# A decoder layer on one core: Toeplitz tiles from zero-padded rows, 128-partition loads, statistics on ScalarE, warm-up products

## The chip, the cores and the metric

One core of a Trainium2 chip runs the whole program. The metric is the device time of one execution in microseconds.

## The reference

x has 4 sequences of 1024 tokens with 256 channels. One pre-norm decoder layer is computed in fp32: a state-space mixer, a cross-attention to 64 context rows, and a feed-forward block with two hidden products of 1024 by 1024. The change touches the mixer alone:

```python
xn = (x - mu) / jnp.sqrt(var + LN_EPS) * ln_gamma + ln_beta   # x is itself layer-normed
dA = jnp.exp(-jnp.exp(log_A) * dt[:, None])                    # 256 channels x 64 states
dB = B_param * dt[:, None]
def step(h, u):
    h = dA * h + dB * u[..., None]
    y = jnp.einsum('dn,bdn->bd', C_param, h) + D_param * u
    return (h, y)
```

The kernel does the scan over time in 16 chunks of 64 tokens. Within a chunk a channel's output is a 64 by 64 lower-triangular Toeplitz matrix times the chunk; between chunks the 64 states are carried.

## The kernel before

Names: tok holds the normed input, 128 partitions (two halves of 64 times, one for each half of the channels) by 64 chunks by 128 channels. GG holds the powers of dA times B times C, built by six doublings on VectorE (L337). EE holds exp of alpha times the position, for the entries into a state. TT, four buffers in the tensor ring, holds Toeplitz tiles of 16 channels each: 64 partitions a half, partition p being the row of kernel values shifted by p.

The rows of kernel values come from TensorE (L461): ones times GG, in four rounds of two banks, evacuated by ScalarE into ksb (L277), stored to DRAM as kernel_rows (L175), 64 values for each of 256 channels, one channel behind the other. tt_load (L141) reads them back for group g, one transfer for each half of the partitions. Since the rows stand close together, the upper triangle holds the next channel's values, and GpSimd sets it to zero (mask, L211, two selects a group). entries_load (L146) reads the alpha rows to all 64 partitions of a half, again one transfer a half.

Order on the queues. SP issues, in program order: coefficients, x in its natural layout (xres), alpha rows out, x by chunks (tok), gamma and beta, EE groups 0 and 1, bo and woT, the eight kernel-row stores (each waits for its evacuation), the later weights' first ones, TT groups 0 to 3, EE groups 2 to 7. TT groups 4 to 7 follow in sync_core, each when the products of a buffer are done; then the feed-forward weights. VectorE does the coefficients, the doublings with statistics (bn_stats, bn_aggr) of x between them, the edit of two rows of GG by D (L397) and its undoing (L411), the norms of 24 of 64 chunks (L370; ScalarE does 40, L284), gamma and beta in eight parts (L379, L384, z_b counts the betas). GpSimd does constants, the powers (1/sqrt), the selects, later the bias.

TensorE's mixer loop runs 17 steps o over 16 octets of 8 channels. Step o does the state products of octet o+1 (L470, EE), the within products of octet o (L477, TT), and the carried products of octet o-1 (L484, GG and the scan of VectorE, L431). It starts with z_b of 3 (L486); at each even step it waits for the mask of a new TT group (L494). The output is evacuated by ScalarE (L304), which between these does the EE exponentials (L289) and the residual's base (L292). Projection, attention and the feed-forward loop of eight blocks follow; none of their lines is changed.

Of the kernel before, what the change touches and what calls it, by code (L numbers as in the profile page):

```python
# [32 lines left out]
P = 128  # L33
# [21 lines left out]
ACT_SHARE = 20  # L55
# [3 lines left out]
def mixer_parts(nc, ctx, a, t):  # L59
# [7 lines left out]
    def sem(name):  # L67
# [12 lines left out]
    ones = sb("ones", [P, 32], "c")  # L80
# [33 lines left out]
    kps = [[pair[k][:, 512 * h:512 * (h + 1)] for h in range(2)] for k in (2, 0)]  # L114
# [5 lines left out]
    const, exps, coef, al_st, coef_t, pk_done, g_row, d_add = (  # L120
        sem("m_" + n) for n in ("const", "exps", "coef", "al_st", "coef_t", "pk_done", "g_row", "d_add"))
    k_ps, k_ev, kr_pad, e_rdy, t_mask = (sem("m_" + n) for n in ("k_ps", "k_ev", "kr_pad", "e_rdy", "t_mask"))
    kr_st = sem("m_kr_st")
    T_in = [sem(f"m_T_in{k}") for k in range(4)]
    stat, aggr, sv_rdy, powd, shift, spr, z_rdy, z_dve, z_h, z_b, natural, nat_v = (
# [13 lines left out]
    def tt_load(e, g):  # L139
        for h in range(2):  # L140
            e.dma_start(TT[g % 4][L * h:L * h + L, :],  # L141
                        bass.AP(t["kr_h"], (8 * h + g) * (GRP * L), [[1, L], [1, GRP * L]])).then_inc(T_in[g % 4], 16)

    def entries_load(e, g):
        for h in range(2):
            e.dma_start(EE[L * h:L * h + L, GRP * g:GRP * g + GRP, :].rearrange("p d n -> p (d n)"),  # L146
                        bass.AP(t["alS_h"], (8 * h + g) * (GRP * N), [[0, L], [1, GRP * N]])).then_inc(E_in[g], 16)

    def sync_mixer(e):
# [20 lines left out]
        for v in range(4):  # L170
            for h in range(2):
                u = 2 * v + h
                e.wait_ge(k_ev, u + 1)
                c = (1 - h) * (P * L) + v * 2048
                e.dma_start(kr[0, c:c + 2048].rearrange("(q m) -> q m", q=4), ksb[0:P:32, u, :]).then_inc(kr_st, 16)  # L175
        for n in ("xW", "keys", "scl"):
            e.dma_start(t[n], a[n]).then_inc(k_in, 16)
        e.wait_ge(kr_st, 128)
        e.wait_ge(kr_pad, 16)
        for g in range(4):  # L180
            tt_load(e, g)
        for g in range(2, NGRP):
            entries_load(e, g)
# [22 lines left out]
    def mask(e, g):  # L206
        e.wait_ge(T_in[g % 4], 32 * (g // 4 + 1))
        for h in range(2):
            e.wait_ge(t_mask, 2 * g + h)
            v = TT[g % 4][L * h:L * h + L, :].rearrange("p (d t) -> p d t", d=GRP)  # L210
            e.affine_select(out=v, in_=v, compare_op=ALU.is_ge, fill=0.0, base=L - 1,  # L211
                            pattern=[[0, GRP], [-1, L]], channel_multiplier=-1).then_inc(t_mask, 1)

# [4 lines left out]
    def gpsimd_prep(e):  # L218
        e.memset(ident[:, :], 0.0).then_inc(const, 1)
        e.memset(rev[:, :], 0.0).then_inc(const, 1)  # L220
        e.memset(ones[:, :], 1.0).then_inc(const, 1)
# [4 lines left out]
        e.wait_ge(const, 6)  # L226
        e.affine_select(out=ident[:, :], in_=ident[:, :], compare_op=ALU.not_equal, fill=1.0, base=0,
                        pattern=[[-1, P]], channel_multiplier=1).then_inc(const, 1)
        for h in range(2):
            blk = rev[64 * h:64 * h + 64, 64 * h:64 * h + 64]  # L230
            e.wait_ge(const, 7 + h)
            e.affine_select(out=blk, in_=blk, compare_op=ALU.not_equal, fill=1.0, base=-63,
                            pattern=[[1, 64]], channel_multiplier=1).then_inc(const, 1)
        e.wait_ge(const, 9)
        e.dma_start(kr[:, DM * L:DM * L + L], rev[0:1, L:2 * L]).then_inc(kr_pad, 16)

        for b in range(2):
# [3 lines left out]
        mask(e, 0)  # L241
        e.wait_ge(t_mask, 2)
        e.wait_ge(nat_v, 1)
        e.tensor_tensor(rsm[:, :], svn[:, :], mhalf[:, :], ALU.pow).then_inc(natural, 1)
        e.wait_ge(natural, 1)
        for g in range(1, 4):
            mask(e, g)
        e.wait_ge(t_mask, 8)

    def gpsimd_core(e):  # L250
        e.wait_ge(wo_in, 32)
        done = 0
        for g, until in ((4, 0), (5, 0), (6, 0), (7, 4), (None, TILES)):
            for tile in range(done, until):
                bias(e, tile)
            done = until
            if g is not None:
                e.wait_ge(base_b, done)
                mask(e, g)
                e.wait_ge(t_mask, 2 * g + 2)  # L260

    def scalar(e):
# [11 lines left out]
        def row_evac(v):  # L274
            e.wait_ge(k_ps, v + 1)
            for h in range(2):
                e.activation(ksb[:, 2 * v + h, :], kps[v % 2][h], ACT.Copy).then_inc(k_ev, 1)  # L277
# [8 lines left out]
        def entry_exp(g):  # L286
            e.wait_ge(E_in[g], 32)
# [5 lines left out]
        for v in range(4):  # L293
            row_evac(v)
        e.wait_ge(const, 9)
        norm_apply(0)
        entry_exp(0)
        norm_apply(1)
        for g in range(1, 3):
# [21 lines left out]
    def vector(e):  # L321
        e.wait_ge(exps, 2)
# [8 lines left out]
        for row in (0, N):  # L331
            e.tensor_copy(edit[row:row + 1, 1, :], wT[row:row + 1, :]).then_inc(d_add, 1)
# [6 lines left out]
        def stats(first, until):  # L339
            for j in range(first, until):  # L340
                if j % 4 == 0:
                    e.wait_ge(xr_in[j // 4], 16)
                e.bn_stats(stn[:, j, :], xres[:, j, :]).then_inc(stat, 1)
                if j % SB >= 2:
                    e.wait_ge(stat, j - 1)
                    e.bn_aggr(mvn[:, j - 2, :], stn[:, j - 2, :]).then_inc(aggr, 1)

        def variances(b):
            for j in (SB * b + SB - 2, SB * b + SB - 1):
                e.wait_ge(stat, j + 1)  # L350
                e.bn_aggr(mvn[:, j, :], stn[:, j, :]).then_inc(aggr, 1)
            e.wait_ge(aggr, SB * b + SB)
# [37 lines left out]
        stats(4, 8)  # L390
        double(5)
        e.wait_ge(d_in, 32)
        e.wait_ge(d_add, 2)
        e.wait_ge(g_row, 7)
        for row in (0, N):
            v = GG[row:row + 1, :, L - 1]
            e.tensor_tensor(v, v, edit[row:row + 1, 0, :], ALU.add).then_inc(d_add, 1)  # L397
        stats(8, 16)
        variances(0)
        stats(16, 26)  # L400
        spreads(0)
        stats(26, 32)
        variances(1)
        e.tensor_scalar(svn[:, :], mvn[:, :, 1], EPS, None, ALU.add).then_inc(nat_v, 1)
        for k in range(2):
            e.memset(hps[k], 0.0).then_inc(h_zero, 1)
        norms(0)
        spreads(1)
        e.wait_ge(k_ps, 4)
        for row in (0, N):  # L410
            e.tensor_copy(GG[row:row + 1, :, L - 1], edit[row:row + 1, 1, :]).then_inc(g_row, 1)  # L411
        e.memset(dec[:, :, 0], 0.0).then_inc(dec0, 1)
        e.wait_ge(bc_in, 64)
        gamma(0)
        norms(1)
        beta(0)
        gamma(1)
        beta(1)
        gamma(2)
# [28 lines left out]
    def tensor(e):  # L448
        e.wait_ge(const, 9)
# [1070 lines left out]
```

## Time and profile before

| what | us |
|---|---|
| median of 3 runs (lowest, highest) | 941.73 (940.8, 942.72) |
| the profiled run's own time | 942.65 |
| its span | 940.9 |
| TensorE matmul busy | 869.4 (92%) |
| VectorE busy | 524.6 (56%) |
| ScalarE busy | 494.1 (53%) |
| GpSimd busy | 184.0 (20%) |

The busy shares are means over stages with different limits. The mixer fills the first 104 us of the span, projection with the first block's attention the next 60, and the feed-forward loop the rest. PE is TensorE's matmul, PEld its weight load, DVE VectorE, ACT ScalarE, POOL GpSimd, SP the engine that issues transfers; a q behind a name is that engine's sequencer. A busy PE is not PE at its peak, since matmuls are pipelined.

### The profile page before, as it was taken

What the parts mean: (1) busy time and instruction counts of PE and PEld (TensorE: products, weight loads), DVE (VectorE), ACT (ScalarE), POOL (GpSimd) and SP (SyncE); (2) the same over time, 40 slices, a digit from 0 to 9 for tenths busy, and PEclk for the clock granted to TensorE, in tenths of its full rate; (3) what the DMA queues carried; (4) which work ended last, traced back from release to release, by engine and by line L of the source; (5) the groups of instructions that cost most, each with busy time, mean ns of one, the idle gap of its engine ahead of it and who ended that gap; (6) DMA issues with size and microseconds to landing.
All of it is one profiled execution on the core that took longest, in us unless ns stands there. A gap on an engine that the chain in (4) does not pass through costs nothing.

```text
span 940.9 us, 15107 instructions
## 1 busy us (share of the span) xinstructions
PE 869.4 (92%) x5570; PEld 695.4 (74%) x5570; DVE 524.6 (56%) x927; ACT 494.1 (53%) x761; POOL 184.0 (20%) x201
## 2 busy tenths in 40 slices
PE   1169899999999999999999999999999999999996
PEld 0068767777877777777777777778777877777885
DVE  7987486646456545646455555555655465544411
ACT  2827533675356635663575446653675357635331
POOL 1667700500050004100220023000500050003000
PEclk9669999999999999999999999999999999999998
DMA  9962797500110011000200020001000110001000
GB/s 346 242 152 52 270 396 280 224 1 1 51 45 0 0 50 45 0 0 22 72 0 0 5 90 0 0 0 64 31 0 0 50 45 0 0 23 46 0 1 24
DMA packets 15496, 61.77 MB, mean 66 GB/s; under 512 B 2835, under 2 KB 4502, under 8 KB 14646
## 3 DMA queue, kind: packets, MB, share of 16 engines
q1 hardware_dynamic: 15430, 61.31, 19.0%
q8 instruction: 23, 0.38, 0.2%
q14 instruction: 11, 0.09, 0.0%
q0 software_dynamic: 32, 0.00, 0.0%
HBM read 49.63 MB, written 23.20 MB: 77 GB/s over the span
## 4 chain that ended last, share of the span: by engine, by line
PE 85%; DVE 7%; issue 4%; ACT 2%; POOL 0%; DMA 0%; DVEq 0%; SPq 0%; ACTq 0%; POOLq 0%
PE pair L1196 50%; PE pair L1183 9%; PE pair L1208 6%; PE pair L1123 4%; PE pair L1134 3%; PE pair L1150 3%; PE pair L470 2%; DVE nat L885 2%; PE pair L1143 1%; PE pair L1173 1%; PE pair L477 1%; PE pair L1090 1%; PE pair L539 1%; PE pair L484 1%; DVE GG L337 1%
## 5 line engine op out<-in xcount | busy, mean ns | idle before, releaser
L806 ACT ACTIVATE vbuf<-pair,scl 128x512 f32<-128x512 f32 x128 | 87.6, 684 | 231.2 <-PE pair L1196 222.3
L1196 PE MATMUL pair<-h2hi,h_turned 128*128 128x512 f32 x512 | 202.6, 396 | 0.0
L1196 PE MATMUL pair<-h2lo,h_turned 128*128 128x512 f32 x512 | 199.6, 390 | 0.0
L1196 PE MATMUL pair<-h1hi,h_turned 128*128 128x512 f32 x384 | 153.1, 399 | 0.0
L1196 PE MATMUL pair<-h1lo,h_turned 128*128 128x512 f32 x384 | 149.9, 390 | 0.0
L973 DVE TENSOR_TENSOR h1lo<-vbuf,h1hi 128x512 fp32r<-128x512 f32 x80 | 57.8, 722 | 119.2 <-ACT h1hi L807 118.4
L1196 PEld LDWEIGHTS pair<-h2hi,h_turned 128*128 128x128 f32 x512 | 96.2, 188 | 25.2 <-issue 5.9
L1196 PEld LDWEIGHTS pair<-h2lo,h_turned 128*128 128x128 f32 x512 | 96.2, 188 | 19.3
L973 DVE TENSOR_TENSOR h2lo<-vbuf,h2hi 128x512 fp32r<-128x512 f32 x64 | 44.2, 691 | 107.2 <-ACT h2hi L807 107.1
L997 DVE SCALAR_TENSOR_TENSOR vbuf<-pair,scl,sg 128x512 f32<-128x512 f32 x64 | 47.4, 748 | 81.7 <-ACT sg L795 69.0
L1183 PE MATMUL pair<-zThi,w_turned 128*128 128x512 f32 x224 | 91.2, 407 | 0.4 <-DVE vbuf L997 0.4
L1196 PEld LDWEIGHTS pair<-h1hi,h_turned 128*128 128x128 f32 x384 | 72.1, 188 | 24.5 <-issue 10.5
L1183 PE MATMUL pair<-zTlo,w_turned 128*128 128x512 f32 x224 | 87.6, 391 | 0.0
L759 ACT ACT_TABLE_LOAD x65 | 83.4, 1283 | 1.2
L700 POOL TENSOR_TENSOR lnv<-lnv 128x4 f32<-128x4 f32 x16 | 16.2, 1015 | 345.1 <-DVE lnv L878 320.4
L1196 PEld LDWEIGHTS pair<-h1lo,h_turned 128*128 128x128 f32 x384 | 72.2, 188 | 14.1
L732 POOL TENSOR_TENSOR h1lo<-vbuf,h1hi 128x512 fp32r<-128x512 f32 x48 | 62.5, 1302 | 82.3 <-ACT h1hi L798 82.3
L795 ACT ACTIVATE sg<-pair,scl 128x512 f32<-128x512 f32 x64 | 43.9, 686 | 58.4 <-PE pair L1183 57.2
L470 PE MATMUL pair<-tok,EE 64*64 64x60 f32 x512 | 38.7, 279 | 26.8 <-DVE tok L384 24.9
L1183 PEld LDWEIGHTS pair<-zThi,w_turned 128*128 128x128 f32 x224 | 42.0, 188 | 15.1 <-DVE vbuf L997 5.0
L714 POOL TENSOR_TENSOR kblk<-keys,hmask 128x256 f32<-128x256 f32 x18 | 10.7, 615 | 207.6 <-PE pair L1123 207.6
L1196 PE MATMUL pair<-h1hi,w_turned 128*128 128x512 f32 x128 | 50.4, 394 | 0.0
(145 smaller groups left out, 1604.3 us busy)
## 6 DMA issues: line engine op xcount, KB each, us to landing
h_turned<-d_h SPq DMA_DIRECT2D x2, 4096.0 KB, 15.0
xres<-in_x SPq DMA_DIRECT2D x8, 512.0 KB, 7.0
tok<-in_xs SPq DMA_DIRECT2D x8, 512.0 KB, 12.1
EE<-alpha_rows SPq DMA_DIRECT2D x16, 256.0 KB, 11.0
ring<-kernel_rows SPq DMA_DIRECT2D x16, 256.0 KB, 4.4
xr<-x_rows SPq DMA_DIRECT2D x8, 512.0 KB, 3.4
out<-xr SPq DMA_DIRECT2D x16, 256.0 KB, 2.1
x_rows<-xres SPq DMA_DIRECT2D x7, 512.0 KB, 11.3
```

Source lines behind the costliest of these rows:

```text
L470: ins = e.matmul(out, EE[L * h:L * h + L, i, :], rhs, start=True, stop=True)
L732: e.tensor_tensor(h1[1][:, m, :], vb[:, m % 2, :], h1[0][:, m, :], ALU.subtract).then_inc(S["lo"], 1)
L759: e.activation(warm[:, 1:2], warm[:, 0:1], function).then_inc(S["warm"], 1)
L795: e.activation(sg[:, m % 2, :], pair[m % 2][:, 0:512], ACT.Silu, scale=sc1[:, m:m + 1]).then_inc(S["sg_rdy"], 1)
L806: e.activation(vb[:, s % 2, :], h_ps[s % 4], ACT.Gelu, scale=sc)
L973: e.tensor_tensor(dst[1][:, n % HC, :], vb[:, n % 2, :], dst[0][:, n % HC, :], ALU.subtract).then_inc(S["lo"], 1)
L997: e.scalar_tensor_tensor(vb[:, m % 2, :], pair[m % 2][:, 512:1024], sc2[:, m:m + 1], sg[:, m % 2, :], ALU.mult, ALU.mult).then_inc(S["v_rd ...
L1123: ins = e.matmul(pair[2][:, g * BLK + b * 256:g * BLK + (b + 1) * 256], qa[64 * g:64 * g + 64, h, tile * P:(tile + 1) * P], kblk[64 * g:64 ...
L1134: ins = e.transpose(pair[3][:, b * BLK + r * P:b * BLK + (r + 1) * P], unit(j, u)[:, r // 2, c:c + P], ident[:, :])
L1183: ins = e.matmul(pair[m % 2][:, 512 * g:512 * g + 512], w[:, k, m * P:(m + 1) * P], zT[part][:, k * BLK:(k + 1) * BLK], start=(k == 0 and ...
L1196: ins = e.matmul(bank, w[:, k, m * P:(m + 1) * P], src[part][:, k, :], start=(k == 0 and part == 0), stop=(k == HC - 1 and part == 1))
L1208: ins = e.matmul(h_ps[m], h1T[:, k, m * P:(m + 1) * P], h1[part][:, k, :], start=(k == 0 and part == 0), stop=(k == HC - 1 and part == 1))
```

## The change

The DRAM rows become 128 values wide (PAD), 64 kernel values and 64 zeros, so that a Toeplitz tile read with a shift of one a partition has its zeros from memory. The selects are gone, and so is their place in GpSimd's later work. The zeros are written once, by four transfers from rev. Each Toeplitz and each EE load is one transfer to 128 partitions whose DRAM side has the counts 2, 64 and the row. Toeplitz tiles grow to 8 KB a partition; two of the four buffers lie in the place of w1 and w2, ksb in that of w3, so the loads of these weights wait for the last within products. The kernel rows are summed over the four rounds into one pair of banks, through a matrix (pick) that has ones in one column, so that round v lands on row v of each block of 32. ScalarE computes mean and variance of tiles 8 to 15 of x by two passes with a summed output each; VectorE does the other 24. The row edits of GG go to GpSimd, their saved copy to ScalarE. Two memsets of banks and one of dec go to the start of VectorE's program. ScalarE does 36 norms and VectorE 28, and norms(1) stands behind gamma and beta of two parts. After the second beta TensorE does five 128x512 products that nothing reads.

```diff
-ACT_SHARE = 20
+ACT_SHARE = 18
+ACT_STATS = (8, 16)
+ROWS_AT = 8
+PAD = 2 * L
...
+    TT = [ring[:, 0:GRP * PAD], ring[:, GRP * PAD:2 * GRP * PAD]]
+    TT += [nc.alloc_sbuf_tensor_at(f"tt{k}", [P, GRP * PAD], F32, offset=t[n])[:, :] for k, n in enumerate(("w1_at", "w2_at"))]
+    ksb = nc.alloc_sbuf_tensor_at("ksb", [P, 2, BLK], F32, offset=t["w3_at"])
...
     def tt_load(e, g):
-        for h in range(2):
-            e.dma_start(TT[g % 4][L * h:L * h + L, :],
-                        bass.AP(t["kr_h"], (8 * h + g) * (GRP * L), [[1, L], [1, GRP * L]])).then_inc(T_in[g % 4], 16)
+        e.dma_start(TT[g % 4], bass.AP(t["kr_h"], g * (GRP * PAD), [[8 * GRP * PAD, 2], [1, L], [1, GRP * PAD]])).then_inc(T_in[g % 4], 16)
 
     def entries_load(e, g):
-        for h in range(2):
-            e.dma_start(EE[L * h:L * h + L, GRP * g:GRP * g + GRP, :].rearrange("p d n -> p (d n)"),
-                        bass.AP(t["alS_h"], (8 * h + g) * (GRP * N), [[0, L], [1, GRP * N]])).then_inc(E_in[g], 16)
+        e.dma_start(EE[:, GRP * g:GRP * g + GRP, :].rearrange("p d n -> p (d n)"),
+                    bass.AP(t["alS_h"], g * (GRP * N), [[8 * GRP * N, 2], [0, L], [1, GRP * N]])).then_inc(E_in[g], 16)
...
+        e.wait_ge(const, 10)
+        for u in range(4):
+            e.dma_start(kr[0, L * u * PAD:L * (u + 1) * PAD].rearrange("(c m) -> c m", m=PAD)[:, L:PAD], rev[0:L, L:P]).then_inc(kr_zero, 16)
         e.wait_ge(al_st, 32)
         for g in range(2):
             entries_load(e, g)
+        for h in range(2):
+            e.wait_ge(k_ev, h + 1)
+            for v in range(4):
+                c = (P * (1 - h) + 32 * v) * PAD
+                e.dma_start(kr[0, c:c + 32 * PAD].rearrange("(q c m) -> q c m", q=4, c=8)[:, :, 0:L],
+                            ksb[v:P:32, h, :].rearrange("q (c m) -> q c m", c=8)).then_inc(kr_st, 16)
+        entries_load(e, 2)
+        e.wait_ge(kr_st, 128)
+        e.wait_ge(kr_pad, 16)
+        e.wait_ge(kr_zero, 64)
+        for g in range(2):
+            tt_load(e, g)
+        entries_load(e, 3)
+        for g in range(2, 4):
+            tt_load(e, g)
+        for g in range(4, NGRP):
+            entries_load(e, g)
...
         e.wait_ge(w_d, 48)
+        e.wait_ge(w_ps, NOCT)
...
+        for row in (0, N):
+            v = GG[row:row + 1, :, L - 1]
+            e.tensor_tensor(v, v, edit[row:row + 1, 0, :], ALU.add).then_inc(d_add, 1)
+        e.wait_ge(d_add, 2)
+        power(0)
+        e.wait_ge(k_ps, 1)
+        e.wait_ge(powd, 1)
+        for row in (0, N):
+            e.tensor_copy(GG[row:row + 1, :, L - 1], edit[row:row + 1, 1, :]).then_inc(g_back, 1)
+        e.wait_ge(g_back, 2)
+        power(1)
...
+        def tile_stats(first, until):
...
+            for j in range(first, until):
+                e.activation(junk[j % 4], xres[:, j, :], ACT.Copy, accum_out=tsum[:, 0, j:j + 1]).then_inc(t_sum, 1)
+            e.wait_ge(t_sum, n)
...
+            for j in range(first, until):
+                e.activation(junk[j % 4], xres[:, j, :], ACT.Square, bias=tsum[:, 1, j:j + 1], scale=1.0 / 16, accum_out=mvn[:, j, 1:2]).then_inc(t_var, 1)
...
+                if c == ROWS_AT:
+                    row_evac()
...
+            if b == 0:
+                e.wait_ge(t_var, ACT_STATS[1] - ACT_STATS[0])
+            e.wait_ge(aggr, ACT_STATS[0] + SB * b)
...
+                    ins = e.matmul(kps[h][32 * q:32 * q + 32, :], pick[N * h:N * h + N, 3 - v:35 - v], GGf[N * h:N * h + N, c:c + 8 * L], start=(v == 0), stop=(v == 3))
+        ins.then_inc(k_ps, 1)
+        e.wait_ge(pk_done, 7)
+        e.wait_ge(w_row, 2)
+        e.wait_ge(z_b, 2)
+        for _ in range(5):
+            e.matmul(pair[3][:, 0:BLK], ident[:, :], GGf[:, 0:BLK], start=True, stop=True)
...
-                e.wait_ge(t_mask, o + 2)
+                e.wait_ge(T_in[o // 2 % 4], 16 * (o // 8 + 1))
```

## Rows read from the trace of the kernel before

**Rows 1.** The page's slices: granted clock and DMA share, in 40 equal slices.
```profile
PEclk9669999999999999999999999999999999999998
DMA  9962797500110011000200020001000110001000
```

**Rows 2.** The chain in order of time: start us, us, what; 0 to 110.
```profile
14.95 4.32 DVE GG L337
...
37.46 1.23 DVE tok L379
...
39.85 1.06 issue
...
46.99 2.17 DVE tok L379
49.19 2.05 DVE tok L384
51.28 1.86 PE pair L470 x30
...
56.64 3.27 issue
```

**Rows 3.** Groups by line, 0 to 104: busy us, mean ns | idle before, releasers.
```profile
L211 POOL TENSOR_SCALAR_AFFINE_SELECT ring<-ring 64x1024 f32<-64x1024 f32 x16 | 24.1, 1508 | 16.5 <-DMA ring<-kernel_rows 15.5
...
L292 ACT ACTIVATE xres<-xres,ngn,rsn 128x256 f32<-128x256 f32 x32 | 17.0, 591 | 0.0
...
L343 DVE BATCH_NORM_STATS2 stn<-xres 128x6 f32<-128x256 f32 x32 | 12.4, 401 | 0.1
...
L370 DVE TENSOR_SCALAR tok<-tok,spread 128x128 f32<-128x128 f32 x24 | 7.9, 406 | 0.0
...
L406 DVE MEMSET pair<- 128x512 f32 x2 | 1.0, 485 | 0.2
...
L397 DVE TENSOR_TENSOR GG<-GG,edit 1x128 f32<-1x128 f32 x2 | 0.8, 404 | 0.2
...
L411 DVE COPY GG<-edit 1x128 f32<-1x128 f32 x2 | 0.6, 300 | 0.1
```

**Rows 4.** Busy time by stretch: us, engines, granted clock, DMA share, GB/s.
```profile
10.00:20.00 10.00, 0.00 (x0) 0.00 (x0) 9.84 (x18) 0.00 (x0) 0.00 (x0) 1.00 1.03 409
50.00:57.00 7.00, 5.35 (x155) 5.13 (x156) 6.97 (x9) 0.00 (x0) 6.61 (x5) 0.61 1.02 230
...
58.00:60.00 2.00, 0.09 (x4) 0.09 (x6) 1.22 (x3) 0.00 (x0) 1.64 (x4) 0.71 0.04 6
```

**Rows 5.** The page's DMA issues: count, KB each, median us to landing.
```profile
EE<-alpha_rows SPq DMA_DIRECT2D x16, 256.0 KB, 11.0
ring<-kernel_rows SPq DMA_DIRECT2D x16, 256.0 KB, 4.4
...
out<-xr SPq DMA_DIRECT2D x16, 256.0 KB, 2.1
...
kernel_rows<-ring SPq DMA_DIRECT2D x8, 8.0 KB
```

**Rows 6.** The tile tok, 0 to 62: its loads, first and last start, landing.
```profile
L161 SPq DMA_DIRECT2D tok<-in_xs x8: 432/447/2067, 7.5 to 12.6; - x8
...
DMA to landing us min/median/max: 9.5/12.1/13.7
```

**Rows 7.** Timeline, one engine at a time: start us, us, what, idle before.
```profile
37.94 2.98 POOL L211 TENSOR_SCALAR_AFFINE_SELECT ring<-ring 64x1024 f32<-64x1024 f32 x2 [3.54 <-DMA ring<-kernel_rows]
...
61.79 1.35 DVE L431 TENSOR_TENSOR_SCAN scan<-dec,pair 128x128 f32<-128x128 f32 x4 [2.57 <-PE pair L484]
...
65.20 1.35 DVE L431 TENSOR_TENSOR_SCAN scan<-dec,pair 128x128 f32<-128x128 f32 x4 [0.94 <-PE pair L484]
...
97.19 1.35 DVE L431 TENSOR_TENSOR_SCAN scan<-dec,pair 128x128 f32<-128x128 f32 x4 [1.82 <-PE pair L484]
...
101.99 1.15 PE L484 MATMUL pair<-scan,GG 64*64 64x64 f32 x32 [0.17 <-PE pair L477]
```

More of the change, by code:

```diff
@@ L79, in mixer_parts @@
     rev = sb("rev", [P, P], "c")
-    ones = sb("ones", [P, 32], "c")
+    pick = sb("pick", [P, 35], "c")
     stn = sb("stn", [P, TILES, 6], "d")
@@ L113, in mixer_parts @@
     yps = [pair[k][:, 512 * h:512 * (h + 1)] for k in (2, 0) for h in range(2)]
-    kps = [[pair[k][:, 512 * h:512 * (h + 1)] for h in range(2)] for k in (2, 0)]
+    kps = [pair[2][:, 512 * h:512 * (h + 1)] for h in range(2)]
+    junk = [pair[0][:, DM * k:DM * (k + 1)] for k in range(4)]
     ident = t["ident"]
@@ L220, in gpsimd_prep @@
         e.memset(rev[:, :], 0.0).then_inc(const, 1)
-        e.memset(ones[:, :], 1.0).then_inc(const, 1)
+        e.memset(pick[:, :], 0.0).then_inc(const, 1)
         e.memset(mhalf[:, :], -0.5).then_inc(const, 1)
@@ L240, in gpsimd_prep @@
             e.tensor_tensor(rn[:, 0, here], sv[:, here], mhalf[:, 0:SB], ALU.pow).then_inc(powd, 1)
-        mask(e, 0)
-        e.wait_ge(t_mask, 2)
+        e.wait_ge(d_in, 32)
+        e.wait_ge(w_row, 2)
+        e.wait_ge(g_row, 7)
+        for row in (0, N):
[9 more added lines that the diff above has]
+        power(1)
         e.wait_ge(nat_v, 1)
+        e.wait_ge(powd, 2)
         e.tensor_tensor(rsm[:, :], svn[:, :], mhalf[:, :], ALU.pow).then_inc(natural, 1)
         e.wait_ge(natural, 1)
-        for g in range(1, 4):
-            mask(e, g)
-        e.wait_ge(t_mask, 8)
     def gpsimd_core(e):
         e.wait_ge(wo_in, 32)
[L252 to L260, printed above, removed]
+        for tile in range(TILES):
+            bias(e, tile)
     def scalar(e):
@@ L292, in residual_base @@
             e.activation(xres[:, j, :], xres[:, j, :], ACT.Identity, bias=ngn[:, j:j + 1], scale=rsn[:, j:j + 1]).then_inc(base, 1)
-        for v in range(4):
-            row_evac(v)
-        e.wait_ge(const, 9)
+        for first in range(*ACT_STATS, 4):
+            tile_stats(first, first + 4)
+        e.wait_ge(const, 10)
         norm_apply(0)
-        entry_exp(0)
         norm_apply(1)
-        for g in range(1, 3):
+        for g in range(3):
             entry_exp(g)
@@ L321, in vector @@
     def vector(e):
+        for k in range(2):
+            e.memset(hps[k], 0.0).then_inc(h_zero, 1)
+        e.memset(dec[:, :, 0], 0.0).then_inc(dec0, 1)
         e.wait_ge(exps, 2)
@@ L389, in vector @@
         double(4)
-        stats(4, 8)
+        stats(4, ACT_STATS[0])
+        last_two(0)
         double(5)
[L392 to L398, printed above, removed]
         variances(0)
-        stats(16, 26)
+        stats(SB, SB + 8)
         spreads(0)
-        stats(26, 32)
+        stats(SB + 8, TILES)
+        last_two(1)
         variances(1)
         e.tensor_scalar(svn[:, :], mvn[:, :, 1], EPS, None, ALU.add).then_inc(nat_v, 1)
-        for k in range(2):
-            e.memset(hps[k], 0.0).then_inc(h_zero, 1)
         norms(0)
         spreads(1)
[L409 to L412, printed above, removed]
         e.wait_ge(bc_in, 64)
         gamma(0)
-        norms(1)
         beta(0)
@@ L418, in vector @@
         beta(1)
+        norms(1)
         gamma(2)
@@ L448, in tensor @@
     def tensor(e):
-        e.wait_ge(const, 9)
+        e.wait_ge(const, 10)
         e.wait_ge(coef, 5)
@@ L476, in within @@
                 rows = slice(L * h, L * h + L)
-                ins = e.matmul(yps[o % 4][rows, c * BC:(c + 1) * BC], TT[o // 2 % 4][rows, (i % GRP) * L:(i % GRP + 1) * L], tok[rows, :, i], start=(c == 0), stop=False)
+                ins = e.matmul(yps[o % 4][rows, c * BC:(c + 1) * BC], TT[o // 2 % 4][rows, (i % GRP) * PAD:(i % GRP) * PAD + L], tok[rows, :, i], start=(c == 0), stop=False)
             return ins
```

83 lines of the change are left out of this document (37 added, 46 removed).

## The prediction

> **What bounds the kernel now.** I read the page's slices first [rows 1]: TensorE's granted clock is at its high level (2.4 GHz) for most of the span but dips towards the low one (1.2 GHz) in the second and third slices, 23 to 71 us, where the DMA row stands at 9 and 6. So this change lives in the first 104 us, the mixer; the feed-forward loop behind it holds none of its lines. Next the chain in order of time [rows 2]. Up to 51.28 it is nearly all VectorE: the doublings of GG (the last at 14.95), the statistics, the norms, gamma and beta. TensorE's mixer products start at 51.28, when the third beta ends, and end at 103.14 [rows 7]. Inside the mixer there is a hole of 3.27 us at 56.64 that the chain calls issue, in which TensorE waits for nothing that the profile shows.
>
> The transfers come next. Between 10 and 20 us all 16 DMA engines are busy and move 409 GB/s; between 50 and 57 us they are as busy and move 230 GB/s [rows 4]. What moves then are the EE loads, 64 partitions each. The ring loads have the same shape, 256 KB each [rows 5]. Nobody waits long for either: of 24.1 us of selects on GpSimd, the idle time before them is 16.5 us, behind DMA [rows 3], and TensorE is held by DVE, not by them.
>
> **The change part by part.** *VectorE loses work ahead of 51.28.* Eight of 32 bn_stats at 401 ns (3.2 us); the two one-row adds (0.8) and the two one-row copies back (0.6), which go to GpSimd; two memsets moved ahead of its first wait (1.0) [rows 3]. The selects also slow VectorE: a stall of 1.06 at 39.85 ends when two selects do, 37.94 + 2.98 [rows 7], and gamma and beta take 2.17 and 2.05 beside selects where one took 1.23 without [rows 2]; without selects that is 1.1 + 0.9 + 0.8 back. Sum 8.4. Four more norms at 406 ns cost 1.6. Net 6.8 us.
>
> *ScalarE gains sixteen passes* over 128x256. No row shows one with a summed output; the nearest plain pass takes 591 ns [rows 3], so they need 9.5 us, or twice that if the sum is a pass of its own. They run beside the doublings, which end at 14.95 + 4.32 = 19.3 [rows 2], and VectorE then waits for them: 0 to 5 us, I take 1. Behind that wait on VectorE stand the statistics of tiles 16 to 31; GpSimd's first power waits with it. The kernel rows come in one accumulated bank pair, two evacuations and not eight. These sit on ScalarE in the middle of its norms, and their eight stores start later than now (they must, since the bank pair is summed to the end). Together TensorE could start some 6 us earlier (2 to 7).
>
> *Warm-up products.* Five products before the third beta, so that the first products find the high clock. The scans step 3.41 us apart (61.79 to 65.20) at the low clock and 2.91 apart over the eleven steps from 65.20 to 97.19 [rows 7]. Three or so low-clock steps give 1.5 us back (0 to 3); if the products run past the third beta they cost 0 to 2.
>
> *The loads.* This is the part that decides. Each EE load becomes one transfer of 128 rows of 4 KB, each Toeplitz load one of 128 rows of 8 KB (the zeros double it, 4.2 MB more in all). Their SBUF side counts 128 partitions, their DRAM side counts 2 by 64, since the two halves lie apart. No transfer of before has such a side. If the rows are dealt out over the engines by the outermost count of both sides, two engines carry all of it. What rows there are: the issues of four rows (kernel_rows from ring) are listed without a time to landing, unlike those of 64 or 128 rows [rows 5], so something else reports for them than for the wide ones. A transfer with an outermost count of two is nearer to four rows than to 64, so I take two engines.
>
> The Trainium skill, "DMA: Bandwidth & Descriptors", in "Why a DMA increments its semaphore by 16 and not by 1", says it outright: the engines used are the largest number up to 16 that divides the slowest count of both sides, which would be 2 here. The same page, in "Rules for kernel authors", asks for one 128-partition transfer in place of two halves, which is the edit; by that sentence alone the loads would run at the 409 GB/s of the early stretch. No run here shows which of them holds for this shape.
>
> Price. One engine at 409/16 = 25.6 GB/s [rows 4]. An EE load, 524,288 bytes over two engines: 10.24 us; a Toeplitz load, 1,048,576 bytes: 20.48 us. Eight of each, one behind the other on the same two: 81.9 + 163.8 = 245.7 us. They start when the tok loads are through, last issue 12.6 plus 13.7 to landing = 26.3 [rows 6]. The queue doesn't run dry: EE groups 0 and 1 last till 47, the kernel-row stores behind them land about 49, EE group 2 covers till 57, and the refills of the four Toeplitz buffers wait on products done long before their turn. bo, woT, xW, keys, scl, vblk and xbo stand ahead of the refills, about 1.05 MB over all engines, 2.6 us at 409 GB/s. A landing adds about 2.1, the time of a 256 KB store [rows 5]. So the eighth Toeplitz load is there at 26.3 + 245.7 + 2.6 + 2.1 = 276.7.
>
> Its wait stands at step 14 of TensorE's mixer loop, and behind it in that queue stands all the rest. From scan 14 (97.19) to the end of the last products (101.99 + 1.15 = 103.14) is 5.95 us now, 2.04 steps; after idling TensorE is at the low clock, so 2.04 times 3.41 = 7.0. The mixer ends at 283.7, not 103.1: plus 180.6. The 6 us at the start, the warm-up and the missing selects are all hidden behind these waits. The other end of the price is 230/16 = 14.4 GB/s an engine [rows 4], the rate of these very loads now: 245.7 becomes 437 and the time about 1315. I take 25.6, since 16 engines writing 64 partitions crowd each other and two don't; the high end keeps a small chance.
>
> *The rest costs nothing in the sum.* Bias, woT and the later weights move back in SP's queue; the added wait of the w1 to w3 loads (products of all 16 octets done) ends with the mixer, before their own wait on the DRAM copies does. Cover gone, they would show in the projection stage.
>
> **The rivals.** (a) *All 16 engines carry the loads.* Then their 12.6 MB move at up to 409 GB/s, the tiles come in time, and the early start counts: 942.65 - 6 - 1.5, and the hole of 3.27 us comes back once more in the denser stretch, +2: about 937 (934 to 941), faster. For it: 128 partitions is the shape of the 409 GB/s stretch; against it: the side that counts 2. It is the other side of zero, and it decides at one point, how many engines share one such load: with four, each load takes half as long, the last lands near 153, and the kernel is still some 60 us slower, so nearly all 16 are needed. (b) *16 engines, but TensorE's code waits behind them.* The hole at 56.64 ends at 59.91, just after the DMA share falls from full to 0.04 in the row of 58 to 60 [rows 2, 4]: it looks like instructions that wait behind data. The new loads last till about the same time, so TensorE would stop earlier and resume at the same 60: no change, 941 to 944. (c) *Two engines at the low rate*: about 1315.
>
> **How the numbers follow.** Span 940.9, profiled run 942.65, median 941.73: the sum is made on 942.65, and the median lies 0.1% under it, which I neglect. Two engines at 25.6 GB/s: 0.62, 1123 us, its own range 1095 to 1170 (rate 27 to 22, landings and order). Rival (a) 0.26, 937. Rival (b) 0.07, 942. Rival (c) 0.05, 1315. The range has to reach to (a), whose chance is over 0.2: from 934, which leaves some 0.09 of (a) below, to 1170, which leaves (c) and a little of the first above. A measurement of this kernel tells about 0.2% from no change. Faster 0.26 from (a); same 0.05 from (b); slower 0.69, 0.02 of it from (b) and 0.67 from the two-engine cases.
>
> **What would show it.** If I am right: EE and ring loads with 20 us and much more from issue to landing; DMA busy about 0.13 and some 51 GB/s from 50 to 270 us; TensorE idle before ring products for some 17 us at every second step, at the low clock; products of group 0 not before 78. Right in any case: no selects, 24 bn_stats on VectorE, z_b reached near 45. Wrong if the EE landings take a few us and the DMA row stays full: then (a) or (b), told apart by the issue holes in TensorE between 46 and 62. Wrong in size if the loads land in step but at another rate.

## The result, and the profile after

The changed kernel takes 1118.5 us (median of 4 runs, 1117.62 to 1119.17), the kernel before, beside it, 942.08 (940.8 to 942.72). The ratio is 1.187, 95% interval 1.1855 to 1.1885: slower by 176 us. The prediction was 1123. The profiled run took 1118.49, its span is 1116.8.

The page's slices, as in [rows 1], now of 27.9 us each:

```profile
PEclk9656555666999999999999999999999999999999
DMA  8111112112994002001100200110020001000000
GB/s 321 53 54 53 54 53 88 55 53 110 327 389 196 1 1 81 0 0 42 38 0 0 80 0 0 42 38 0 0 66 14 0 36 44 0 0 38 19 1 20
```

From the second slice to the ninth the DMA row stands at 1 or 2 and the rate at 53 to 55 GB/s, except for 88 in the seventh, in which SP issues the loads of bo, woT and the later weights; TensorE's clock is near its low level (1.2 GHz) for all of that time. The windows, with the columns of [rows 4], give the same in numbers:

```profile
10.00:20.00 10.00, 0.00 (x0) 0.00 (x0) 10.00 (x21) 7.89 (x36) 0.80 (x2) 1.00 1.03 408
...
46.00:100.00 54.00, 7.08 (x230) 6.95 (x232) 7.20 (x17) 2.89 (x3) 0.00 (x0) 0.54 0.13 53
...
200.00:272.00 72.00, 19.52 (x610) 19.11 (x612) 8.12 (x24) 12.46 (x23) 11.21 (x16) 0.64 0.13 53
```

A share of 0.13 is 2.1 of 16 engines. Over two engines 53 GB/s is 26.5 each, where the early stretch has 408 over 16, so 25.5 each. That is the work of two engines at full speed; which engines they are these rows don't say. The page's DMA issues fit it (count, KB each, median us to landing):

```profile
EE<-alpha_rows SPq DMA_DIRECT2D x8, 512.0 KB
ring<-kernel_rows SPq DMA_DIRECT2D x4, 1024.0 KB
tt<-kernel_rows SPq DMA_DIRECT2D x4, 1024.0 KB
```

In [rows 5] the halves had a time to landing; these have none, like the stores of four rows there.

Where the time went is read from TensorE's timeline in the mixer (start us, us, what, idle before and what ended it):

```profile
37.61 5.91 PE L491 MATMUL pair<-GG,ident 128*128 128x512 f32 x10 [12.12 <-DVE tok L421]
43.70 1.86 PE L499 MATMUL pair<-tok,EE 64*64 64x60 f32 x32 [0.18 <-DVE tok L421]
77.90 0.36 PE L499 MATMUL pair<-tok,EE 64*64 64x60 f32 x2 [32.34 <-DMA ring<-kernel_rows]
97.75 0.36 PE L499 MATMUL pair<-tok,EE 64*64 64x60 f32 x2 [15.02 <-DMA ring<-kernel_rows]
127.68 0.36 PE L499 MATMUL pair<-tok,EE 64*64 64x60 f32 x2 [23.67 <-DMA tt<-kernel_rows]
147.53 0.36 PE L499 MATMUL pair<-tok,EE 64*64 64x60 f32 x2 [13.39 <-DMA tt<-kernel_rows]
160.35 0.36 PE L499 MATMUL pair<-tok,EE 64*64 64x60 f32 x2 [9.14 <-ACT tok L333]
211.51 0.36 PE L499 MATMUL pair<-tok,EE 64*64 64x60 f32 x2 [47.77 <-DMA ring<-kernel_rows]
231.35 0.37 PE L499 MATMUL pair<-tok,EE 64*64 64x60 f32 x2 [13.85 <-DMA ring<-kernel_rows]
251.20 0.36 PE L499 MATMUL pair<-tok,EE 64*64 64x60 f32 x2 [13.59 <-DMA tt<-kernel_rows]
271.03 0.36 PE L499 MATMUL pair<-tok,EE 64*64 64x60 f32 x2 [13.53 <-DMA tt<-kernel_rows]
...
275.90 1.54 PE L513 MATMUL pair<-scan,GG 64*64 64x64 f32 x38
```

Eight waits, one for each Toeplitz group: 32.34 + 15.02 + 23.67 + 13.39 + 47.77 + 13.85 + 13.59 + 13.53 = 173.2 us. The longest, 47.77, falls where the EE loads of groups 4 to 7 stand ahead of the fifth Toeplitz load. The 9.14 at 160.35 stand behind ScalarE, which itself waits 47.66 us there for an EE load; they lie ahead of that Toeplitz load and put off nothing. The mixer ends at 275.90 + 1.54 = 277.44 in place of 103.14 [rows 7], 174.3 us later, which leaves 1.5 of the 175.8 between the two profiled runs for all the rest.

The front of the kernel did what was forecast. Statistics on VectorE (DVE) and ScalarE (ACT), each by line, with count, busy time and mean ns, and three rows of VectorE's timeline:

```profile
L374 DVE BATCH_NORM_STATS2 stn<-xres 128x6 f32<-128x256 f32 x24 | 9.2, 399 | 0.0
```

```profile
L300 ACT ACTIVATE pair<-xres,tsum 128x256 f32<-128x256 f32 x8 | 3.7, 462 | 0.1
L294 ACT ACTIVATE pair<-xres 128x256 f32<-128x256 f32 x8 | 3.0, 372 | 0.1
...
L294 ACT ACTIVATION_READ_ACCUMULATOR pair<-xres 128x1 f32 x8 | 1.5, 189 | 0.0
```

```profile
14.54 4.41 DVE L368 TENSOR_TENSOR GG<-GG,pk 128x4096 f32<-128x4096 f32 x1
18.86 0.17 DVE L391 TENSOR_SCALAR sv<-mvn 128x16 f32<-128x16 f32 x1
...
42.41 1.23 DVE L421 TENSOR_TENSOR tok<-tok,bet 128x1024 f32<-128x1024 f32 x1
```

L391 waits for ScalarE's sums and starts as the last doubling ends: ScalarE held nobody up. The five warm-up products (L491, listed as ten) end at 43.52 and the third beta at 43.64; the first state products follow at 43.70, 7.6 us before the 51.28 of [rows 2].

### The profile page after: what moved, and what is told of

Its sections match the earlier page's. It is cut to its first block, busy times and chain, and to the rows that moved or that the text cites. A ratio compares the mean times of both kernels' runs of the same rounds, so it can differ in the third digit from the quotient of the medians.

```text
span 1116.8 us, 15109 instructions
## 1 busy us (share of the span) xinstructions
PE 881.5 (79%) x5580; PEld 705.1 (63%) x5580; DVE 513.6 (46%) x909; ACT 498.6 (45%) x789; POOL 160.7 (14%) x190
## 4 chain that ended last, share of the span: by engine, by line
PE 70%; SPq 13%; DMA 5%; DVE 4%; issue 3%; another core or an unknown queue 2%; ACT 2%; POOL 0%; DVEq 0%; ACTq 0%; POOLq 0%
PE pair L1225 42%; PE pair L1212 7%; SPq L150 7%; PE pair L1237 5%; DMA ring<-kernel_rows 4%; SPq L147 3%; PE pair L1152 3%; PE pair L1163 2%; PE pair L1179 2%; DVE nat L914 2%; PE pair L1172 1%; PE pair L1202 1%; PE pair L1119 1%; SPq L179 1%
## 5 line engine op out<-in xcount | busy, mean ns | idle before, releaser
L499 PE MATMUL pair<-tok,EE 64*64 64x60 f32 x512 | 42.6, 292 | 182.5 <-DMA ring<-kernel_rows 109.0
L499 PEld LDWEIGHTS pair<-tok,EE 64*64 64x64 f32 x512 | 33.5, 195 | 184.7 <-DMA ring<-kernel_rows 109.6
L457 DVE TENSOR_TENSOR_SCAN scan<-dec,pair 128x128 f32<-128x128 f32 x64 | 21.7, 401 | 199.5 <-PE pair L513 166.7
L333 ACT ACTIVATE tok<-pair 128x512 f32<-128x512 f32 x16 | 9.3, 588 | 105.7 <-PE pair L513 105.7
```

The costliest lines, as they stand in the source:

```text
L499: ins = e.matmul(out, EE[L * h:L * h + L, i, :], rhs, start=True, stop=True)
```

## The experiments

"Split" means a load in two transfers of 64 partitions, as before the change; "the split kernel" is the changed kernel with both kinds of load split. Where a load becomes two transfers or one, the counts of the waits for it change with it; the diffs leave these lines out.

**Undo the merged loads, all else as changed.**

```diff
-        e.dma_start(TT[g % 4], bass.AP(t["kr_h"], g * (GRP * PAD), [[8 * GRP * PAD, 2], [1, L], [1, GRP * PAD]])).then_inc(T_in[g % 4], 16)
+        for h in range(2):
+            e.dma_start(TT[g % 4][L * h:L * h + L, :],
+                        bass.AP(t["kr_h"], (8 * h + g) * (GRP * PAD), [[1, L], [1, GRP * PAD]])).then_inc(T_in[g % 4], 16)
...
-        e.dma_start(EE[:, GRP * g:GRP * g + GRP, :].rearrange("p d n -> p (d n)"),
-                    bass.AP(t["alS_h"], g * (GRP * N), [[8 * GRP * N, 2], [0, L], [1, GRP * N]])).then_inc(E_in[g], 16)
+        for h in range(2):
+            e.dma_start(EE[L * h:L * h + L, GRP * g:GRP * g + GRP, :].rearrange("p d n -> p (d n)"),
+                        bass.AP(t["alS_h"], (8 * h + g) * (GRP * N), [[0, L], [1, GRP * N]])).then_inc(E_in[g], 16)
```

> The changed kernel, with every Toeplitz load and every EE load as two transfers of 64 partitions each; everything else stays as changed (zeros in memory, 8 KB a partition, statistics on ScalarE, warm-up). Theory, two engines carry a transfer whose DRAM side counts 2 outermost: the loads run on all 16 again, the last Toeplitz load lands long before its step (about 80 us and not 270.6), the DMA share between 46 and 56 us is near full, the mixer ends where the early start puts it, 7.6 us ahead of before less what the loads cost: 935 us (931 to 941). Rival, the doubled bytes and not the engines are the cause: 4.2 MB more at the 230 GB/s of before are 18 us, and the time would be 950 to 965. Rival, something other than these two loads holds the mixer: above 1050, with TensorE still waiting for the ring 17 us at a time.

954.2 us, ratio 1.011 (1.0091 to 1.0128). 164 of the 176 us are gone, so the two merged loads are the cause of nearly all. But the time is in the rival's range (950 to 965), 1.1% above the kernel before, although the first products start at 45.22. TensorE's waits between 44 and 113 us (us in all, times, longest), and its timeline:

```profile
PE pair L509 <- issue: 17.6, 5, 4.8
PE pair L516 <- issue: 2.6, 1, 2.6
```

```profile
61.55 0.37 PE L509 MATMUL pair<-tok,ring 64*64 64x64 f32 x2 [4.43 <-issue]
...
70.20 0.27 PE L509 MATMUL pair<-tok,tt 64*64 64x64 f32 x1 [4.41 <-issue]
...
79.69 0.37 PE L509 MATMUL pair<-tok,tt 64*64 64x64 f32 x1 [4.80 <-issue]
```

No wait names a load. These are stops like the one of 3.27 us in [rows 2], of which the kernel before has 5.6 us in the same stretch. The windows (DMA share and GB/s are the last two columns) show full engines under them:

```profile
46.00:78.00 32.00, 17.45 (x517) 16.60 (x513) 15.26 (x32) 6.43 (x10) 4.15 (x6) 0.79 1.04 241
```

In the trace one packet of 16 KB of the instruction queue starts at 49.89, at 58.86, at 67.41 and at 76.76; the four longest stops end at 52.73, 61.55, 70.20 and 79.69, each 2.7 to 2.9 us later. Three of these packets start 1.6 to 1.9 us into the stop; between 97 and 113 us, where the engines are no longer full, such packets start and TensorE doesn't stop. In the kernel before the packet starts at 57.12 and the stop ends at 59.91, 2.8 later. So it looks as if TensorE runs out of code, and the packet with the next piece starts late while the data fill the engines. What a packet holds the profile doesn't say; whether the stops depend on the transfers is tested below.

**One of the two merged loads alone.** Only EE split (the second half of the diff above):

> The changed kernel, with only the EE loads as two transfers of 64 partitions; the Toeplitz loads stay one transfer of 128. Theory of two engines: the eight Toeplitz loads stay in series on the same two engines, 8 x 19.9 us from about 46 us, with the EE loads' sixteenth (some 10 us in all) between them: the last lands near 215 (210 to 225) and not at 270.6, and the time is 1118.5 - 56 = 1063 us (1045 to 1080). Theory that one kind of load alone is to blame: 935 if it is EE, 1118 if it is the Toeplitz loads.

1061.71 us (1.1252, 1.1228 to 1.1277). The forecast of 1063 holds, and its path too: the last Toeplitz load lets TensorE go at 214.59, forecast 215.

```profile
214.59 0.36 PE L500 MATMUL pair<-tok,EE 64*64 64x60 f32 x2 [13.58 <-DMA tt<-kernel_rows]
```

```profile
55.73 20.41 SPq L147 DMA_DIRECT2D tt<-kernel_rows  x2
76.19 34.11 SPq L151 DMA_DIRECT2D EE<-alpha_rows  x8
```

These are issues on SP's queue (start, us, count). SP itself is held 34.11 us by the issues of eight EE halves, which took 0.6 us each where all loads were split; the likely reason is that two of their 16 engines are full of Toeplitz rows. The fifth Toeplitz load lets TensorE go at 155.07, in the changed kernel at 211.51.

Only the Toeplitz loads split (the first half):

> The changed kernel, with only the Toeplitz loads as two transfers of 64 partitions; the EE loads stay one transfer of 128. Theory of two engines: 8 x 10.1 us of EE loads in series from 26.7 us, with a sixteenth of the Toeplitz bytes (8 x 2.5 us) and the store of the kernel rows between them: the last EE load lands at 118 to 130 us, four steps of 3.3 us follow, the mixer ends near 138 and the time is about 975 us (955 to 985). Theory that one kind of load alone is to blame: 935 if it is the Toeplitz loads, 1118 if it is EE.

1010.01 us (1.0711, 1.0687 to 1.0735), 35 above the forecast. Both kinds of load cost, each by itself, so the theory of two engines stands, but the working missed a step. TensorE's longest wait and SP's queue:

```profile
147.88 0.36 PE L501 MATMUL pair<-tok,EE 64*64 64x60 f32 x2 [39.96 <-DMA ring<-kernel_rows]
```

```profile
70.67 37.42 SPq L152 DMA_DIRECT2D EE<-alpha_rows  x4
...
127.50 3.38 SPq L148 DMA_DIRECT2D ring<-kernel_rows  x4
```

What held the mixer was not the last EE load but the fifth Toeplitz load: it goes over 16 engines, but SP could issue it only at 127.50, after 37.42 us in the EE issues and some 19 in those behind them. From its issue to TensorE's go another 20.4 us pass. Packets of 4 KB, the size of EE rows, still move till about 134 us, so the share of the load on the two engines of EE likely stood behind them; no run separates this from the late issue.

**The kernel before with EE merged, nothing else.**

```diff
-        for h in range(2):
-            e.dma_start(EE[L * h:L * h + L, GRP * g:GRP * g + GRP, :].rearrange("p d n -> p (d n)"),
-                        bass.AP(t["alS_h"], (8 * h + g) * (GRP * N), [[0, L], [1, GRP * N]])).then_inc(E_in[g], 16)
+        e.dma_start(EE[:, GRP * g:GRP * g + GRP, :].rearrange("p d n -> p (d n)"),
+                    bass.AP(t["alS_h"], g * (GRP * N), [[8 * GRP * N, 2], [0, L], [1, GRP * N]])).then_inc(E_in[g], 16)
```

> The kernel before, with one part of the change alone: each EE load is one transfer of 128 partitions. Theory of two engines: 8 x 10.1 us from about 26 us plus a sixteenth of the other bytes (some 12 us): the last EE load lands at 112 to 125 us, the mixer ends near 133 in place of 103, the time is about 970 us (955 to 985). Rival, one 128-partition transfer in place of two halves is no loss by itself (it hurts only with the doubled rows): 940 to 943.

995.2 us (1.0547, 1.0524 to 1.057): 51 us from this edit alone, 25 above the forecast, with the same picture. SP is in the issues of six EE loads from 55.92 on, for 43.02 us, and TensorE waits 34.78 us for the selects on the fifth Toeplitz group, which was issued at 110.78:

```profile
133.74 0.36 PE L469 MATMUL pair<-tok,EE 64*64 64x60 f32 x2 [34.78 <-POOL ring L210]
```

```profile
55.92 43.02 SPq L145 DMA_DIRECT2D EE<-alpha_rows  x6
...
110.78 10.85 SPq L141 DMA_DIRECT2D ring<-kernel_rows  x8
```

**Is it the outermost count, or the one transfer?** The kernel with Toeplitz loads split and EE merged (1010.0), with the alpha rows stored eight times:

```diff
-                    bass.AP(t["alS_h"], g * (GRP * N), [[8 * GRP * N, 2], [0, L], [1, GRP * N]])).then_inc(E_in[g], 16)
+                    bass.AP(t["alS_h"], g * (GRP * N), [[P * N, 16], [0, 8], [1, GRP * N]])).then_inc(E_in[g], 16)
...
-            e.dma_start(alS[P * (1 - u):P * (2 - u), :], al2[:, u, :]).then_inc(al_st, 16)
+            e.dma_start(alS[8 * (1 - u):8 * (2 - u), :].rearrange("r (d n) -> d r n", n=N),
+                        al2[:, u, :].unsqueeze(1).to_broadcast([P, 8, N])).then_inc(al_st, 16)
```

> The kernel with Toeplitz loads in two halves and each EE load one transfer of 128 partitions (1010.0 us), with one size changed: the alpha rows are stored eight times for each half, so that the DRAM side of the same EE load counts 16 by 8 and not 2 by 64. Theory, the outermost count of the DRAM side sets the number of engines: an EE load is carried by 16 engines, its 4 KB packets take about 160 ns (as in the early x loads to 128 partitions) and not 281 (as in the halves), EE is through in some 10 us in all, TensorE never waits for it, and only the stops for code remain, fewer than in the split kernel (954.2), since 7.6 us of full transfers are gone: 948 us (942 to 956). Rival, one transfer of 128 partitions is slow by itself, or the reading of one row many times is: 1005 to 1015.

955.26 us (1.013, 1.011 to 1.0151), from 1010: in the forecast range, 7 above its middle. The same transfer of 128 partitions, with 16 in place of 2 as the outermost count of its DRAM side, is carried by all engines; its times to landing are there again, for the tile EE:

```profile
DMA to landing us min/median/max: 5.0/17.1/26.9
```

The other half of the expectation falls: the rate. It is 954.2 with EE in halves and 955.3 with EE in one, and the window 62 to 70, EE loads among others, moves no more than the halves did:

```profile
62.00:70.00 8.00, 4.75 (x127) 4.57 (x127) 4.94 (x10) 3.21 (x5) 0.00 (x0) 0.50 1.03 236
```

**Both loads in one transfer over 16 engines.** The Toeplitz rows are copied eight times a half:

```diff
+        for h in range(2):
+            e.dma_start(bass.AP(t["kc_h"], L + 8 * h * KX, [[KX - 8, 8], [1, KX - 8]]),
+                        bass.AP(t["kr_h"], h * P * PAD, [[0, 8], [1, KX - 8]])).then_inc(kr_copy, 16)
+        e.wait_ge(kr_copy, 32)
...
-        e.dma_start(TT[g % 4], bass.AP(t["kr_h"], g * (GRP * PAD), [[8 * GRP * PAD, 2], [1, L], [1, GRP * PAD]])).then_inc(T_in[g % 4], 16)
+        e.dma_start(TT[g % 4], bass.AP(t["kc_h"], L + g * (GRP * PAD), [[KX, 16], [1, 8], [1, GRP * PAD]])).then_inc(T_in[g % 4], 16)
```

> The changed kernel with its one-transfer loads of 128 partitions, both from DRAM sides that count 16 by 8: the alpha rows stored eight times a half, the padded kernel rows copied from DRAM to DRAM eight times a half, each copy 8 values less far on. Theory: 12.6 MB at 409 GB/s are 31 us in place of 245.7 on two engines; the copies stand ahead of the first Toeplitz load and cost 5 to 8 us there, so it lands at 43 to 47, about when the first products are ready; some stops for code stay: 938 us (932 to 945). Rival, a copy from DRAM to DRAM runs on few engines: 526 KB on two are 20 us, the first Toeplitz load lands near 60, 950 to 960. Rival, 128 partitions in one transfer are slow by themselves: above 1100.

960.14 us (1.0178, 1.0157 to 1.0199), not 938. The time is at the end of the first rival's range, but not for its reason. The copies were as quick as forecast (both there by 43.05), but the loads behind them run at 222 GB/s and not at 409, so TensorE waits for the first and stops for code as before:

```profile
50.00:66.00 16.00, 9.99 (x320) 9.77 (x322) 6.79 (x17) 2.34 (x3) 0.00 (x0) 0.71 1.01 222
```

```profile
51.76 0.36 PE L506 MATMUL pair<-tok,EE 64*64 64x60 f32 x2 [5.37 <-DMA ring<-kernel_copies]
```

**Do the stops come from the transfers?** The split kernel with the loads of groups 4 to 7 cut to a sixteenth:

```diff
+            n = GRP * PAD if g < 4 else PAD
...
+            n = GRP if g < 4 else 1
...
+        e.memset(EE[:, 4 * GRP:, :], 0.0).then_inc(const, 1)
...
```

> The split kernel, with the loads of groups 4 to 7 cut to a sixteenth (one channel of 16 in each EE and Toeplitz load; GpSimd sets the rest of EE to zero beforehand). Left out: the entries and Toeplitz tiles of 15 in 16 channels of these groups, so the output of half the channels is not the reference's; the instructions of TensorE are the same. 954.2 with whole loads, where TensorE stands still five times for 17.6 us in all, for issue and not for a load. Theory, TensorE's code waits behind the data on the DMA engines: the transfers then end near 57 us, the stop of 2.6 us at 49.9 stays, the one at 57 shortens to about 2, and the later three, some 10.6 us, vanish: 941 us (938 to 945). Rival, the stops have nothing to do with the transfers (order of the waits, the two halves' weights, the clock): five stops stay and the time is 951 to 955.

943.7 us (1.0004, 0.9994 to 1.0014), in the range of the theory. The stops fall from 20.5 to 9.4 us in all. The engines are full to 66 us and not to 57, with the first products put off to 47.2, probably by GpSimd's zeros, and two long stops lie in that stretch (4.18 and 4.01); behind it none is over 0.33, where the split kernel had some thirteen us. So the stops depend on the transfers, and that rival falls:

```profile
40.00:66.00 26.00, 16.89 (x304) 12.76 (x306) 15.45 (x35) 7.68 (x13) 1.26 (x7) 0.76 1.02 225
66.00:100.00 34.00, 32.81 (x1148) 31.68 (x1144) 23.24 (x54) 23.99 (x42) 20.74 (x28) 0.96 0.06 13
```

**Fewer bytes, zeros from memory.** Split loads, Toeplitz tiles read in pieces of 64 values:

```diff
-                        bass.AP(t["kr_h"], (8 * h + g) * (GRP * PAD), [[1, L], [1, GRP * PAD]])).then_inc(T_in[g % 4], 16)
+                        bass.AP(t["kr_h"], (8 * h + g) * (GRP * PAD), [[1, L], [PAD, GRP], [1, L]])).then_inc(T_in[g % 4], 16)
...
```

> The split kernel, with Toeplitz tiles of 64 values a channel read out of the 128-value rows in pieces of 256 bytes (zeros still from memory, no selects, 4 KB a partition, four buffers in the ring). 4.2 MB less. Theory, TensorE's code waits behind the data: 6.3 MB in place of 8.4 are queued ahead of the first steps, the DMA engines are through near 59 us, two stops of 2.6 and 4.4 stay of 17.6: 943 us (939 to 948). Rival, pieces of 256 bytes cost more than they save: their bound is the stores of such pieces at 18 ns each, 14 GB/s an engine, beside 15 for the 8 KB rows now; were they twice as slow, the transfers would end where they end now and the time would stay at 952 to 958.

942.56 us (0.9999, 0.9987 to 1.0011). The forecast of 943 holds in the time, but not by its working alone: the stops fall from 20.5 to 11.8 us where 17.6 were to fall to 7, and the first products come 1.5 us earlier than in the split kernel (43.75 against 45.22). From 45.67 (first scan, before: 53.33) to 99.71 (last scan, before: 100.31) a lead of 7.7 us shrinks to 0.6.

The same with EE groups 4 to 7 issued inside the loop, after the products of octets 0, 2, 4, 6:

```diff
-        for g in range(4, NGRP):
-            entries_load(e, g)
...
+            e.wait_ge(w_ps, 2 * (g - 4) + 1)
+            entries_load(e, g)
             e.wait_ge(w_ps, 2 * (g - 4) + 2)
             tt_load(e, g)
```

> As the one with pieces of 256 bytes, and the EE loads of groups 4 to 7 are each issued one step into the mixer's loop (after the products of octets 0, 2, 4, 6) and not in one go. Theory, code behind data: 4.2 MB are queued ahead, the DMA engines are through near 51 us and idle between the later loads, so one stop of some 2.6 us stays: 939 us (935 to 943). Rival, an EE load comes too late for ScalarE's exponential, which stands ahead of the next evacuation: TensorE then waits for ScalarE, 943 to 950.

942.18 us (0.9992, 0.9978 to 1.0006), just inside the range, no different from before. Two long stops stay, not one, and a third of 1.63:

```profile
56.93 0.37 PE L508 MATMUL pair<-tok,ring 64*64 64x64 f32 x2 [2.87 <-issue]
64.02 0.26 PE L508 MATMUL pair<-tok,ring 64*64 64x64 f32 x1 [2.76 <-issue]
```

Without the five warm-up products:

```diff
-        for _ in range(5):
+        for _ in range(0):
             e.matmul(pair[3][:, 0:BLK], ident[:, :], GGf[:, 0:BLK], start=True, stop=True)
```

> As the paced one, without the five warm-up products. In the split kernel the third beta ended at 43.79 and the warm-up at 45.29, so it held TensorE 1.5 us; the first steps would then go at the low clock, 3.41 and not 2.91 us each, for three or four steps. If both are so, the time is the same within 1 us (937 to 941). If the warm-up is worth its place: 2 us longer. If it does nothing for the clock: 1.5 us shorter.

941.28 us (0.9984, 0.9975 to 0.9994), 0.9 us under the paced kernel: inside the 1 us, 0.3 above the range that was named. The warm-up gives no more than it costs: without it the first products start at 44.06 and not at 44.70, and the clock then stands at 0.50 until 50 in place of 1.00.

EE from the eightfold rows (the edit of the run on the outermost count) with the Toeplitz pieces:

> The kernel with Toeplitz pieces of 256 bytes in two halves (942.6 us), with the EE loads as one transfer of 128 partitions from eightfold alpha rows. Theory, 128 partitions and 16 engines together move the EE bytes at 409 and not 235 GB/s: 7.6 us of full transfers less, of its stops for code (2.1, 4.6 and three short ones) the long one vanishes: 938 us (934 to 942). Rival, the stops don't depend on how long the engines are full but on whether they are full at 48 to 50 and 54 to 58: 941 to 944.

944.75 us (1.0024, 1.0013 to 1.0034), where 938 was forecast; the rival's range, 941 to 944, is nearer. The forecast's premise was the 409 GB/s, which the two runs with 16 engines above refute; it was written before their results.

**One load at a time.** On the paced kernel, each load behind the sixth waits for the landing of the one before:

```diff
+            e.wait_ge(T_in[(g - 1) % 4], 32 * ((g - 1) // 4 + 1))
             e.wait_ge(w_ps, 2 * (g - 4) + 1)
             entries_load(e, g)
+            e.wait_ge(E_in[g], 32)
             e.wait_ge(w_ps, 2 * (g - 4) + 2)
             tt_load(e, g)
...
```

> The paced kernel with pieces of 256 bytes (942.2 us, two stops for issue of 2.9 and 2.8 us at 54 and 61), in which, after the first three EE and two Toeplitz loads and EE group 3, SP issues each load only when the one before has landed, and the loads of bo, woT and the later weights go behind Toeplitz groups 5 and 7. Theory, TensorE's code waits behind the transfers that are queued ahead of it: then at most one load of about 2.5 us is ahead of a code fetch, the two stops shrink to under 1 us each, and the early start of some 6 us is kept at last: 938 us (935 to 941). Rival, loads one at a time are too slow: ten of them at 2.2 us and 2 us to landing are 42 us beside 14 steps of 3 us, so TensorE waits for a load by name or for ScalarE's exponential behind one, 1 to 6 us in all: 942 to 948. Rival, the stops aren't made by the transfers: they stay, 942.

949.67 us (1.0072, 1.0058 to 1.0086), where 938 was forecast; it is even above the first rival's range. Both parts show. The stops that are left for code are short, 4.5 us in all, and the scan of octet 11 starts at 81.09, where the kernel before has 88.46. Then the loads come too late: ScalarE waits 28.1 us for EE in four waits, and TensorE behind it 12.3 in three, the longest 8.72.

```profile
58.04 0.27 PE L514 MATMUL pair<-tok,ring 64*64 64x64 f32 x1 [1.82 <-issue]
72.61 0.30 PE L514 MATMUL pair<-tok,ring 64*64 64x64 f32 x2 [1.03 <-issue]
89.69 0.36 PE L507 MATMUL pair<-tok,EE 64*64 64x60 f32 x2 [8.72 <-ACT tok L341]
```

```profile
ACT EE L327 <- DMA EE<-alpha_rows: 28.1, 4, 10.2
```

So a lead of 7.4 us was kept for eleven octets; a pace between the two was not tried, and no kernel here beats the one before by more than 0.2%.

## Why the prediction was right, step by step

- *The engine count.* Two, as taken. The share of 0.13 and the 53 GB/s were forecast as 0.13 and 51, and the same transfer with a count of 16 runs on all engines. The first within products stand at 77.90, forecast not before 78. The times to landing that were to show it too are not listed. The Trainium skill, "DMA: Bandwidth & Descriptors", "Why a DMA increments its semaphore by 16 and not by 1", states this rule (the largest number up to 16 that divides the slowest counts of both sides), and the traces agree for the two counts that were run: 53 GB/s with 2, 236 with 16. The advice of the Trainium skill, same page, "Rules for kernel authors", to use one transfer of 128 partitions was worth nothing here even with 16 engines: 955.3 against 954.2 us.
- *The price.* 25.6 GB/s an engine was forecast, 26.5 measured. Groups 6 and 7 of the Toeplitz tiles let TensorE go at 251.20 and 271.03, 19.8 us apart, forecast 20.5; eight times that difference is most of the 5.7 us by which the last came earlier than the 276.7 forecast. Where no EE load lies between, the wait from one Toeplitz load to the next is 13.4 to 15.0 us and not some 17, since two steps of work lie between them and not one; the sum didn't use this.
- *The tail.* 271.03 to 277.44 is 6.4 us, forecast 7.0. Mixer end 277.4, forecast 283.7.
- *No dry queue.* The step held, but not only for the reason given. SP itself stands still: single issues of these loads take up to 20 us, probably since the queues of their two engines are full.

```profile
54.44 20.14 SPq L150 DMA_DIRECT2D EE<-alpha_rows  x1
74.62 29.52 SPq L147 DMA_DIRECT2D tt<-kernel_rows  x2
104.18 60.01 SPq L150 DMA_DIRECT2D EE<-alpha_rows  x4
```

  In the whole change this alters nothing, since the loads are in series anyway. In the single edits of EE the forecasts lacked it and missed by 25 and 35 us.
- *The start.* 7.6 us earlier, forecast 6 (2 to 7): ScalarE's statistics cost no wait where 1 was taken, their sixteen passes with their sums 9.7 us where 9.5 was taken. Gamma and beta, 2.17 and 2.05 beside selects [rows 2], took 1.22 and 1.23, as the sum had it. Of the 1.6 us over the forecast, 0.6 have no account. None of this shows in the time of the changed kernel, as forecast; no run undoes these parts one by one.
- *Rival (a) was priced wrongly.* With all 16 engines it was to give 937. It gives 954 with the loads split and 960 with both in one transfer. Two terms were mis-sized: the rate (409 taken, 241 measured, so the 12.6 MB fill the engines for 52 us and not 31) and the stops for code (2 us more taken, 20.5 in place of 5.6 measured). Rival (b) had the mechanism, TensorE's code behind the data, but its end, no change, held only with the smaller Toeplitz reads. So the prediction was wrong that the sign hangs on the engine count: with all 16 engines the changed kernel is slower too, by 1 to 2%. That the sign was safe on this side as well was luck.
- *A reason that fell.* The prediction put the low rate of the loads before, 230 GB/s [rows 4], down to 16 engines writing 64 partitions. With 128 partitions over 16 engines it is 222 to 236. What these loads share is that many partitions read the same few rows of DRAM; no run separates that from other causes, so it stays open.

## What to carry to other kernels

Before two halves are merged into one transfer, look at the outermost count of both sides: where the DRAM side stepped over two blocks, the transfer ran on two engines, though it filled 128 partitions. Such transfers also held up the engine that issues them, and everything queued behind them. An early start is worth only what the transfers leave of it: in long full stretches of DMA TensorE stopped, probably for its code, for as long as the gain or longer.

## What was unexpected of the hardware

- In a full DMA stretch, and just behind one, TensorE stops without any wait on data: 5.6 us in all in the mixer before, 20.5 in the split kernel, 4.5 with one load at a time. The stops of over 2 us end 2.5 to 3.0 us after the start of a 16 KB packet of the instruction queue. The Trainium skill, "Runtime: NRT & Kernel Launch", "Instruction fetch mechanics", describes that queue (blocks of 16 KiB, 256 instructions, fetched ahead) and calls its cost mostly hidden. Here that holds where the engines are not full: with a DMA share of 0.06 from 66 us on, the kernel with the small loads has no stop over 0.33 us there.
- An issue on SP took 0.6 us for a load in two halves, and up to 20.14 us for one that two engines carry.
- Sixteen engines read these DRAM rows, in packets of 4 and 8 KB, at 222 to 241 GB/s, into 64 or 128 partitions, one transfer or two, from one copy or eight; two engines read them at 53, and 16 engines read x at 408.
